# A graph and mixing layer with routed experts: group sizes, early row addresses and unused TensorE products between its two halves

## The chip, the cores and the metric

The kernel runs on one core of one Trainium2 chip. The metric is the device time of one execution in microseconds (us). The engines named below are TensorE (PE), VectorE (DVE), ScalarE (ACT), GpSimd (POOL) and SyncE (SP), which only issues transfers here. Engines wait for one another on semaphores: `x.wait_ge(s, v)` stops engine x until semaphore s has reached v.

## The reference

```python
xn = layernorm(x)                                    # x: 6250 x 256
x = x + gnn(xn, edges) + mix(xn)                     # graph part; linear attention of 8 heads
f = layernorm(x)
logits = softmax(relu(f @ rw1 + rb1) @ rw2 + rb2)    # 6 experts
top_w, top_i = top_k(logits, 2); w = softmax(top_w)
e_out = three layers of 256 x 256 per expert (relu, relu, none), with biases
x = x + sum over the 2 chosen experts of w * e_out
```

## The kernel before

The 6250 rows lie as 50 tiles of 125 rows. The **mixing part** goes through them in 25 pairs. For pair i TensorE forms the mixing product (`mix`), DVE adds the graph rows and x (`mixed_rows`, L1027), and the layernorm and the router follow on ACT, PE and DVE over the next four steps of the loop. Pairs are collected in seven **groups**, `SIZES = (4, 5, 4, 4, 3, 3, 2)`. When the last pair of a group is through the router, DVE chooses the two experts of each of its rows and ranks them (`route`, in four parts: part 0 two steps after that pair, parts 1 and 2 three steps after it, part 3 four steps after it; between parts 2 and 3 TensorE sums the ranks, `ranks`). Part 3 ends with the positions of the rows (L1094, L1095). POOL then writes each tile of the group, 125 rows, to its place in a table `tab0` sorted by expert: one indirect transfer (**scatter**, L588) for each tile, so two for each pair. So groups 4, 5 and 6 (counted from 0) end with pairs 19, 22 and 24 and are 6, 6 and 4 scatters.

After the last group TensorE forms the counts of rows per expert (L1341), DVE turns them into ends of regions (`fill`, L1124) and into two lists, first for the table of first choices, then for that of second choices: the first row of each block of 128 rows (`tab_row`, L1140, signalled as `tab_done`) and its expert (`tab_e`, L1142, signalled as `e_done`). SP writes seven blocks of empty rows behind the regions, six of them after `fill` is ready (`fill_up`, L474).

The **expert part** takes blocks of 128 rows, two to a step, 27 steps for first choices and 27 for second choices. For each block SP reads its address from `tab_row` into a register (`value_load`, L488) and issues the transfer of its rows (L497) into one of 14 buffers; semaphore `r_in` tells that both blocks have landed. ACT normalises them (L775), PE turns them (transposes, L1351), ACT and DVE split them into a high and a low half (L790, L1170), and PE computes the three layers of a step, each two blocks of six products (L1359 to L1361), layers of neighbouring steps interleaved. DVE adds biases (L1150) and weights the result (L1158). POOL writes the rows of a first-choice step into the second table (`second_rows`, L599, two transfers) and adds the results to the output (`add_rows`, L610, two transfers). POOL's order is written out: `second_rows` of steps 0 to 7, then `add_rows(n)` and `second_rows(n + 8)` in turn. Before SP issues the rows of step 27, the first of the second choices, it waits for the last `second_rows`.

Before its first rows SP waits in this order: for the first list (`tab_done`), for the empty blocks of the first table (`fill_out[0]`), and for the scatters and the output writes of the last four groups. It issues nothing else in between.

Of the kernel before, what the change touches and what calls it, by code (L numbers as in the profile page):

```python
# [16 lines left out]
E, F, RH = 6, 256, 128  # L17
# [14 lines left out]


Q = 10
SIZES = (4, 5, 4, 4, 3, 3, 2)
ENDS = tuple(sum(SIZES[:g + 1]) for g in range(len(SIZES)))
GROUPS = len(SIZES)
RB = 4
# [4 lines left out]
HB = 2  # L43
REG = N + S
# [28 lines left out]
def tiles_of(g):  # L73
    return range(2 * (ENDS[g] - SIZES[g]), 2 * ENDS[g])


def gps_layer(nc, x, src, dst, w_kv, w_q, w_oT, b_out, w_g, a_l, a_r, rw1, rb1, rw2, rb2,
              ew1, eb1, ew2, eb2, ew3, eb3, out):
    ctx = ExitStack()
    with ctx:  # L80
        def sb(name, shape, dt=FP32):
            return ctx.enter_context(nc.sbuf_tensor(name, shape, dt))

        def sem(name):
            return ctx.enter_context(nc.semaphore(name))
# [44 lines left out]
        mix_h, mix_l = wg_h[:, :, 0:D], wg_l[:, :, 0:D]  # L130
# [79 lines left out]
        tab_row = sb("tab_row", [1, 2, NTT], I32)  # L210
# [30 lines left out]
        d_ps = ctx.enter_context(nc.psum_tensor("d_ps", [128, 512], FP32))  # L241
# [49 lines left out]
        sc_out, x2_out = [sem(f"sc_out{b}") for b in range(RB)], [sem(f"x2_out{b}") for b in range(RB)]  # L291
        we_in, be_in, b3_in = sem("we_in"), sem("be_in"), sem("b3_in")

        cnt_done, tstep, tab_done, e_done, fill_out = sem("cnt_done"), sem("tstep"), sem("tab_done"), sem("e_done"), [sem(f"fill_out{k}") for k in range(2)]
        fill_ready, second_out = sem("fill_ready"), [sem(f"second_out{c}") for c in range(CB)]
        r_in = [sem(f"r_in{u}") for u in range(U)]
# [23 lines left out]
        def scattered(g):  # L320

            return 16 * sum(2 * SIZES[a] for a in range(g % RB, g + 1, RB))

        def stored(g):

            return 32 * sum(SIZES[a] for a in range(g % RB, g + 1, RB))

# [9 lines left out]
        def expert_regs(engine, name):  # L337
            return [[engine.alloc_register(f"{name}{h}_{i}") for i in range(EL * HB)] for h in range(SETS)]
# [14 lines left out]
        def has(n):  # L353
            return 0 <= n < ALL

        def added(n):

            return z_out[n % YB], 16 * HB * (n // YB + 1)

        def copied(n):  # L360

            return second_out[n % CB], 16 * HB * (n // CB + 1)
# [5 lines left out]
        def _(sp):  # L368
# [100 lines left out]
            def fill_up(k):  # L469
                tab = (tab0, tab1)[k]  # L470
                sp.load(end_regs, fill[0:1, k, 0:E])
                for reg in end_regs:
                    end = sp.snap(reg, min_val=0, max_val=(E - 1) * REG + N)
                    sp.dma_start(tab[bass.ds(end, S), :], skip_rows[:, :]).then_inc(fill_out[k], 16)  # L474

            fill_up(0)
            sp.wait_ge(tab_done, 1)
            sp.wait_ge(fill_out[0], 16 * (E + 1))
            for g in range(GROUPS - RB, GROUPS):
                sp.wait_ge(sc_out[g % RB], scattered(g))  # L480
                sp.wait_ge(x2_out[g % RB], stored(g))

            for n in range(ALL):
                k, j = n // PAIRS, n % PAIRS
                if n == PAIRS:
                    sp.wait_ge(tab_done, 2)
                for h in range(HB):
                    first = sp.value_load(tab_row[0:1, k, j * HB + h:j * HB + h + 1], min_val=0, max_val=E * REG)  # L488
                    if h == 0 and n >= U:
                        sp.wait_ge(*added(n - U))  # L490
                        if n - U < PAIRS:
                            sp.wait_ge(*copied(n - U))
                    if n == PAIRS and h == 0:
                        sp.wait_ge(fill_out[1], 16 * (E + 1))
                        for m in range(PAIRS - CB, PAIRS):
                            sp.wait_ge(*copied(m))
                    sp.dma_start(rb[n % U][:, h, :], (tab0, tab1)[k][bass.ds(first, S), :]).then_inc(r_in[n % U], 16)  # L497
                if n == U - 1:
                    fill_up(1)
# [4 lines left out]
        def _(pool):  # L504
# [80 lines left out]
            for g in range(GROUPS):  # L585
                pool.wait_ge(row_ready, g + 1)
                for j in range(2 * SIZES[g]):
                    pool.indirect_dma_start(out=tab0, out_offset=bass.IndirectOffsetOnAxis(ap=pos0[:, g % RB, j:j + 1], axis=0),  # L588
# [595 lines left out]
        def _(pe):  # L1184
# [159 lines left out]
            pe.wait_ge(we_in, 32 * E)  # L1344
            pe_e = expert_regs(pe, "pe_e")

            def turned(outp, rows):

                for h in range(HB):
                    for c in range(KC):  # L1350
                        last = pe.transpose(outp[:, h, c, :], rows[:, h, c * 128:(c + 1) * 128], ident[:, :])  # L1351
                return last

            def expert_layer(outp, layer, hi, lo, e):

                at = e * EW + layer * LW
                for c in range(KC):
                    w = bass.ds(at + c * F, F)
                    pe.matmul(outp, hi[:, c, :], we_h[:, w], start=c == 0, stop=False)  # L1359
                    pe.matmul(outp, hi[:, c, :], we_l[:, w], start=False, stop=False)  # L1360
                    last = pe.matmul(outp, lo[:, c, :], we_h[:, w], start=False, stop=c == KC - 1)  # L1361
                return last

            def step(n, es):
                if has(n):
                    pe.wait_ge(in_l_done, n + 1)
                    for h in range(HB):
                        last = expert_layer(l1_ps[:, h, :], 0, in_h[:, h, :, :], in_l[:, h, :, :], es[n, h])
                    last.then_inc(l1_done, 1)
                if has(n - 1):  # L1370
                    pe.wait_ge(h1_l_done, n)
                    for h in range(HB):
                        last = expert_layer(l2_ps[:, h, :], 1, h1_h[:, h, :, :], h1_l[:, h, :, :], es[n - 1, h])
                    last.then_inc(l2_done, 1)
                if has(n + 1):
                    pe.wait_ge(xe_done, (n + 2) * HB)
                    turned(tin_ps, xe[:, (n + 1) % 2, :, :]).then_inc(tin_done, 1)
                if has(n):
                    pe.wait_ge(hs1_done, (n + 1) * HB)
                    turned(th1_ps, hs1).then_inc(th1_done, 1)  # L1380
                if has(n - 2):
                    m = n - 2
                    pe.wait_ge(h2_l_done, m + 1)
                    if m >= 2:
                        pe.wait_ge(y_done, (m - 1) * HB)
                    for h in range(HB):
                        last = expert_layer(l3_ps[m % 2][:, h, :], 2, h2_h[:, h, :, :], h2_l[:, h, :, :], es[m, h])
                    last.then_inc(l3_done, 1)
                if has(n - 1):
                    pe.wait_ge(hs2_done, n * HB)  # L1390
                    turned(th2_ps, hs2).then_inc(th2_done, 1)

            tiles(pe, pe_e, step)


# [28 lines left out]
```

## Time and profile before

| | us |
|---|---|
| median of 3 runs | 745.61 (744.7 to 746.4) |
| the profiled execution's own time | 744.4 |
| its span, first to last instruction | 742.6 |

```profile
PE 666.2 (90%) x4705; PEld 615.6 (83%) x4705; DVE 555.0 (75%) x1427; ACT 446.1 (60%) x879; POOL 449.4 (61%) x392
PE   3999999999999988988874299999999999999993
PEclk9999999999999999899985599999999999999998
```

The first line gives busy time, share of the span and instructions of each engine. The other two cut the span in 40 slices of 18.6 us: tenths of busy time of PE (9 is 90% or more), and the TensorE clock that was granted, in tenths of full speed. Before the two low slices lies the mixing part, behind them the expert part.

### The profile page before, as it was taken

Reading aid. Unit: us, or ns where it says so; the run is one execution under the profiler, and the core shown is the slowest. Engines: PE = TensorE matmul, PEld = TensorE weight load, DVE = VectorE, ACT = ScalarE, POOL = GpSimd, SP = SyncE. Lnnn points to the kernel's source line nnn. Section 1 sums busy time; section 2 is a strip of 40 time slices with the busy share of each in tenths; the row PEclk is TensorE's granted clock in tenths of the full one; section 3 lists DMA queues with packets and bytes.
Section 4 is the critical chain, followed back from the end, with each engine's and each line's share of the span. In section 5 each row is a group of like instructions: output and inputs, shape, how many; then the busy total and the mean of one; then the engine's idle time right before and its main releaser. Section 6 shows DMA issues by size and latency. Waiting matters only on the chain.

```text
span 742.6 us, 15734 instructions
## 1 busy us (share of the span) xinstructions
PE 666.2 (90%) x4705; PEld 615.6 (83%) x4705; DVE 555.0 (75%) x1427; ACT 446.1 (60%) x879; POOL 449.4 (61%) x392
## 2 busy tenths in 40 slices
PE   3999999999999988988874299999999999999993
PEld 2888888888888777867663289999999999999993
DVE  5785788888888787678777167777777777777773
ACT  2666577777777547567771166566566566656651
POOL 3465788766666200535466478888888865555555
PEclk9999999999999999899985599999999999999998
DMA  8954544444443367768554578666646965554443
GB/s 229 270 159 145 164 130 125 129 123 122 123 125 110 111 226 241 238 212 267 186 137 115 142 201 187 133 122 119 111 83 108 173 112 95 88 94 60 46 46 36
DMA packets 80759, 104.79 MB, mean 141 GB/s; under 512 B 21156, under 2 KB 62456, under 8 KB 80679
## 3 DMA queue, kind: packets, MB, share of 16 engines
q1 hardware_dynamic: 48135, 70.98, 32.2%
q0 software_dynamic: 32544, 32.80, 25.3%
q8 instruction: 43, 0.70, 0.4%
q14 instruction: 37, 0.30, 0.2%
HBM read 53.35 MB, written 52.26 MB: 142 GB/s over the span
## 4 chain that ended last, share of the span: by engine, by line
PE 79%; DVE 10%; ACT 3%; POOL 2%; issue 2%; DMA 2%; SPq 1%; POOLq 0%; DVEq 0%; ACTq 0%
PE kv_ps L1359 10%; PE kv_ps L1360 10%; PE kv_ps L1361 10%; PE pt L1351 6%; PE d_ps L1223 6%; PE kv_ps L1200 5%; PE kv_ps L1203 5%; PE kv_ps L1201 5%; PE xt_ps L1351 3%; PE kv_ps L1300 2%; PE pt L1200 2%; PE pt L1203 2%; PE pt L1201 2%; POOL tab L588 1%; PE pt L1291 1%
## 5 line engine op out<-in xcount | busy, mean ns | idle before, releaser
L1359 PE MATMUL kv_ps<-we_h,now_h 128*128 x648 | 192.7, 297 | 3.6 <-DVE now_l L1170 2.0
L1360 PE MATMUL kv_ps<-we_l,now_h 128*128 x648 | 183.5, 283 | 0.0
L1361 PE MATMUL kv_ps<-we_h,now_l 128*128 x648 | 183.5, 283 | 0.0
L1359 PEld LDWEIGHTS kv_ps<-we_h,now_h 128*128 128x128 f32 x648 | 124.2, 192 | 5.0 <-issue 5.0
L1360 PEld LDWEIGHTS kv_ps<-we_l,now_h 128*128 128x128 f32 x648 | 124.5, 192 | 0.0
L1361 PEld LDWEIGHTS kv_ps<-we_h,now_l 128*128 128x128 f32 x648 | 124.0, 191 | 0.0
L1150 DVE TENSOR_TENSOR work<-kv_ps,be 128x256 f32<-128x256 f32 x216 | 81.5, 419 | 50.5 <-PE kv_ps L1361 50.1
L610 POOL DMA_INDIRECT out_x<-work,arena x56 | 87.6, 1565 | 39.7 <-DVE work L1158 26.9
L790 ACT ACTIVATE now_h<-pt 128x512 fp32r<-128x512 f32 x54 | 32.5, 602 | 103.3 <-PE pt L1351 103.3
L556 POOL DMA_INDIRECT alg<-xt_tab,src_all x50 | 63.1, 1261 | 38.9 <-DVE arena L939 17.4
L962 DVE TENSOR_REDUCE ss<-xring 125x16 f32<-125x1040 f32 x50 | 61.8, 1236 | 19.9 <-ACT xring L675 18.3
L559 POOL DMA_INDIRECT arena<-xt_tab,dst_all x50 | 61.5, 1230 | 15.2 <-issue 15.2
L1223 PEld LDWEIGHTS d_ps<-work 125*128 125x128 f32 x400 | 52.0, 191 | 4.8 <-DVE work L976 0.9
L1170 DVE TENSOR_TENSOR now_l<-pt,now_h 128x512 fp32r<-128x512 f32 x54 | 37.3, 691 | 23.5 <-ACT now_h L790 23.4
L775 ACT ACTIVATE staged<-arena 128x256 f32<-128x256 f32 x80 | 43.5, 597 | 18.5 <-DMA arena<-tab 18.5
L588 POOL DMA_INDIRECT tab<-work,pos x14 | 16.9, 1206 | 62.1 <-DVE work L1095 58.4
L1223 PE MATMUL d_ps<-work 125*128 125x128 f32 x400 | 52.5, 275 | 0.7 <-DVE work L976 0.7
L599 POOL DMA_INDIRECT tab<-arena x40 | 40.3, 1008 | 21.0 <-issue 10.7
L1200 PE MATMUL kv_ps<-wkv_h,x_h 128*128 128x512 f32 x120 | 49.7, 414 | 0.6 <-ACT arena L648 0.6
L588 POOL DMA_INDIRECT tab<-arena,pos x24 | 28.8, 1200 | 32.9 <-DVE arena L1095 26.5
L1351 PE MATMUL pt<-ident,staged 128*128 128x128 f32 x216 | 33.3, 278 | 16.9 <-ACT staged L775 16.9
L1201 PE MATMUL kv_ps<-wkv_l,x_h 128*128 128x512 f32 x120 | 47.0, 392 | 0.0
(253 smaller groups left out, 1826.4 us busy)
## 6 DMA issues: line engine op xcount, KB each, us to landing
arena<-tab SPq DMA_DIRECT2D x80, 131.0 KB, 3.1
xring<-in_x SPq DMA_DIRECT2D x29, 224.0 KB
we_h<-wt_h SPq DMA_DIRECT2D x6, 768.0 KB, 6.0
we_l<-wt_l SPq DMA_DIRECT2D x6, 768.0 KB, 8.6
xt_tab<-arena SPq DMA_DIRECT2D x7, 577.5 KB
weight_in<-tab SPq DMA_DIRECT2D x28, 131.0 KB, 2.6
out_x<-arena SPq DMA_DIRECT2D x12, 224.0 KB
staged<-in_ew SPq DMA_DIRECT2D x9, 256.0 KB, 4.6
```

The lines of the kernel that those rows point to most:

```text
L556: pool.indirect_dma_start(out=alg[:, b, t % CH, :], out_offset=None, in_=xt_tab, in_offset=bass.IndirectOffsetOnAxis(ap=src_all[:, t:t + 1 ...
L559: pool.indirect_dma_start(out=xtg[:, b, t % CH, :], out_offset=None, in_=xt_tab, in_offset=bass.IndirectOffsetOnAxis(ap=dst_all[:, t:t + 1 ...
L610: pool.indirect_dma_start(out=out, out_offset=bass.IndirectOffsetOnAxis(ap=rb[u][:, h, C_TOK:C_TOK + 1].bitcast(I32), axis=0), in_=yw[n % ...
L962: dve.reduce_sum(ss[:, t % 2, :], sq[t % 2], axis=AX.X).then_inc(red_done, 1)
L1150: dve.tensor_tensor(rows[:, h, :], outp[:, h, :], be[layer][:, bass.ds(es[n, h] * F, F)], ALU.add).then_inc(finished, 1)
L1200: pe.matmul(outp, x_h[:, t, c, :], w_h(c), start=c == 0, stop=False)
L1201: pe.matmul(outp, x_h[:, t, c, :], w_l(c), start=False, stop=False)
L1223: last = pe.matmul(d_ps[:, at], vs[t % VB][:, at], ks[t % VB][:, at], start=False, stop=t == T - 1, skip_group_check=True)
L1351: last = pe.transpose(outp[:, h, c, :], rows[:, h, c * 128:(c + 1) * 128], ident[:, :])
L1359: pe.matmul(outp, hi[:, c, :], we_h[:, w], start=c == 0, stop=False)
L1360: pe.matmul(outp, hi[:, c, :], we_l[:, w], start=False, stop=False)
L1361: last = pe.matmul(outp, lo[:, c, :], we_h[:, w], start=False, stop=c == KC - 1)
```

## The change

The groups become `(4, 5, 5, 4, 3, 2, 2)`: group 2 has five pairs in place of four, and group 5 two in place of three, so groups 2, 3 and 4 end one pair later than before and groups 5 and 6 as before. SP reads the addresses of the first two blocks before its waits for the last scatters. TensorE issues products whose result nobody reads: 40 when the first list of experts is ready, 24 when the scatters of the last group have landed, 8 when the rows of step 0 have landed, and 10 behind the transposes of step 0. They have 128 x 128 weights and 256 columns, the shape of the mixing part's and the layers' products, and write the upper half of the bank `d_ps`.

```diff
-SIZES = (4, 5, 4, 4, 3, 3, 2)
+SIZES = (4, 5, 5, 4, 3, 2, 2)
...
             sp.wait_ge(fill_out[0], 16 * (E + 1))
+            early = [sp.value_load(tab_row[0:1, 0, h:h + 1], min_val=0, max_val=E * REG) for h in range(HB)]
             for g in range(GROUPS - RB, GROUPS):
                 sp.wait_ge(sc_out[g % RB], scattered(g))
                 sp.wait_ge(x2_out[g % RB], stored(g))
...
-                    first = sp.value_load(tab_row[0:1, k, j * HB + h:j * HB + h + 1], min_val=0, max_val=E * REG)
+                    first = early[h] if n == 0 else sp.value_load(tab_row[0:1, k, j * HB + h:j * HB + h + 1], min_val=0, max_val=E * REG)
...
             pe.wait_ge(we_in, 32 * E)
             pe_e = expert_regs(pe, "pe_e")
 
+            def idle_products(count):
+
+                for i in range(count):
+                    pe.matmul(d_ps[:, F:2 * F], wg_h[:, 0, 0:128], mix_h[:, 1, :], start=True, stop=True)
+
+            pe.wait_ge(e_done, 1)
+            idle_products(40)
+            pe.wait_ge(sc_out[(GROUPS - 1) % RB], scattered(GROUPS - 1))
+            idle_products(24)
+            pe.wait_ge(r_in[0], 16 * HB)
+            idle_products(8)
+
...
                     turned(tin_ps, xe[:, (n + 1) % 2, :, :]).then_inc(tin_done, 1)
+                if n < 0:
+                    idle_products(10)
                 if has(n):
```

## Rows read from the trace of the kernel before

**Rows 1.** Busy time by stretch: us, busy (instructions) per engine, granted clock, DMA share.
```profile
386.00:398.00 12.00, 9.61 (x33) 7.30 (x33) 6.75 (x36) 6.38 (x14) 6.68 (x6) 0.56 0.61 168
408.00:420.80 12.80, 0.00 (x0) 0.02 (x1) 2.62 (x9) 1.09 (x2) 3.70 (x4) 0.50 0.47 121
420.80:428.00 7.20, 5.51 (x23) 4.72 (x24) 1.54 (x4) 2.17 (x4) 5.44 (x6) 0.50 0.64 180
429.00:440.00 11.00, 10.59 (x88) 10.12 (x88) 7.74 (x16) 7.54 (x17) 7.89 (x9) 1.00 0.73 205
```

**Rows 2.** Chain of work that ended last: start us, us, what.
```profile
395.46 0.27 DVE rk L1091
...
396.94 1.18 POOL tab L588
...
410.63 4.71 DMA tab<-weight_in,pos
415.49 0.28 SPq L488
...
416.28 0.37 SPq L497
...
417.43 2.06 DMA arena<-tab
419.57 1.10 ACT staged L775 x2
...
420.81 1.10 PE pt L1351 x4
...
424.04 0.21 PE kv_ps L1360
...
430.43 0.12 PE kv_ps L1359
...
431.87 0.45 PE pt L1351 x4
```

**Rows 3.** TensorE in order of time: start us, us, line, tile, idle before.
```profile
423.46 0.58 PE L1359 MATMUL kv_ps<-we_h,now_h 128*128 x1 [1.57 <-DVE now_l L1170]
...
428.74 0.38 PE L1359 MATMUL kv_ps<-we_h,now_h 128*128 x1 [0.29 <-DVE now_l L1170]
```

**Rows 4.** DVE in order of time, end of the mixing part and the lists.
```profile
326.78 0.69 DVE L1027 TENSOR_TENSOR arena<-kv_ps,y 125x512 f32<-125x512 f32 x1
...
384.00 0.69 DVE L1027 TENSOR_TENSOR weight_in<-kv_ps,y 125x512 f32<-125x512 f32 x1
...
388.52 0.21 DVE L1069 TENSOR_REDUCE tw<-kv_ps 125x6 f32<-125x48 f32 x1 [2.58 <-PE kv_ps L1315]
...
404.23 0.16 DVE L1124 CAST fill<-d_ps 1x16 int32<-1x16 f32 x1
...
408.09 0.63 DVE L1142 TENSOR_SCALAR tab_e<-gsum_sb 1x54 int32<-1x54 f32 x1
```

**Rows 5.** POOL in order of time: group 4's first scatter, steps 0 and 26.
```profile
384.18 1.19 POOL L588 DMA_INDIRECT tab<-work,pos  x1 [4.71 <-DVE work L1095]
...
420.31 1.01 POOL L599 DMA_INDIRECT tab<-arena  x1 [8.49 <-DMA arena<-tab]
...
562.42 1.01 POOL L599 DMA_INDIRECT tab<-weight_in  x1 [0.30 <-issue]
```

**Rows 6.** SP's empty blocks in order of time, and the last one's landing.
```profile
406.04 3.68 SPq L474 DMA_DIRECT2D tab<-skip_rows  x6
...
L474 SPq DMA_DIRECT2D tab<-skip_rows x1: 772/772/772, 409.0 to 409.0; - x1
DMA to landing us min/median/max: 4.1/4.1/4.1
```

**Rows 7.** Step 27's rows on ACT, and what TensorE's weight loads waited for.
```profile
568.87 1.09 ACT L775 ACTIVATE staged<-weight_in 128x256 f32<-128x256 f32 x2 [1.25 <-DMA weight_in<-tab]
...
572.07 0.42 PEld L1351 LDWEIGHTS pt<-ident,work 128*128 128x128 f32 x4 [0.20 <-DVE work L1150]
```

## The prediction

> **What bounds the kernel now.** I read first the busy time by stretch [rows 1]: from 408.00 to 420.80 us TensorE does nothing, from 420.80 to 428.00 it works at a granted clock of 0.50, and from 429 on it is busy without a break at 1.00. So the change aims at a hole of some 17 us in which TensorE waits, and at 7 us at half speed behind it. The chain of waits [rows 2] says what fills the hole: the first scatter of group 5 starts at 396.94, the last of group 6 at 410.63, ten without a break, and the last one lands 4.71 us after its start, at 415.34. Then SP reads an address (415.49), issues (416.28), and the second block's transfer starts at 417.43, 1.94 us after the first read. It lands at 419.49, ACT takes 1.10 us, and TensorE's transposes start at 420.81.
>
> Last I looked for what else could set the end, and found POOL. From its first `second_rows` at 420.31 to the last one at 562.42 [rows 5] it works through 27 `second_rows` and 19 `add_rows` with hardly more than its 0.30 us between two transfers. SP can load step 27 only behind that last one, and ACT waits 1.25 us for these rows; DVE falls behind with it, and TensorE's weight loads wait 0.20 us for DVE [rows 7]. **TensorE has no reserve there.** What TensorE gains beyond what POOL gains is paid back at step 27.
>
> **Part 1, the groups.** Group 5 loses two scatters of 1.5 us ((410.63 - 396.94) / 9 = 1.52). That isn't a gain of 3.0, since group 4 now ends a pair later: its part 3 moves from ahead of the 25th pair's L1027 (384.00) to behind it. Of the steps moved for groups 2 and 3, I add up the intervals between the twelve L1027 from 326.78 to 384.00 [rows 4] in the new order of plain and routing pairs: 57.5 in place of 57.2 us, so the last pair starts 0.24 later, at 384.24. On TensorE its ranks now stand directly ahead of the router products that DVE waited for until 388.52, so I take the ranking for 388.3, and the first scatter follows 1.48 us behind the ranking (395.46 to 396.94, rows 2), at 389.8. Before it was at 384.18 [rows 5]. From there the queue is full: 14 scatters, 13 x 1.50 = 19.5, and 0.25 for those that SP's issues slow down. The last starts at 409.55 and lands 4.7 later, at 414.25: **1.1 us earlier**. Bounds: nothing (group 4 or 6 late by 1.1) and 3.0 (both scatters saved whole).
>
> What that move costs: DVE's hole of 2.58 us ahead of 388.52 [rows 4] hid nothing before; now the ranks go ahead of these router products on TensorE, and part 3 ahead of part 0 of group 5 on DVE. Part 0 comes up to 1.2 later; parts 1 to 3 of group 5 with four rows in place of six give back about 0.5. I take 0.7 us for everything behind: the ends (404.23), the list of experts (408.09 + 0.63, so 409.4 in place of 408.7) and the empty blocks; bounds 0.2 and 1.5. Group 6's scatters are ready at 404.2 and POOL comes to them at 404.8, so this doesn't show there.
>
> **Part 2, the addresses.** Both reads leave the way behind the last landing. From the first read to the second transfer's issue it was 1.94 us; left are two issues of 0.37 each, some 0.5. But the reads stand behind the wait for the empty blocks. Their last issue is at 409.0 and lands at 413.1 [rows 6]; 0.7 later is 413.8. Two reads (0.79 from the first one's start to its issue, of which I take 0.6 for the read itself) end at 415.0, and that is behind the scatters' landing at 414.25. So this wait takes the place of the one removed: issues at 415.2 and 415.65, against 417.43: 1.8 earlier. If the scatters gained nothing, the issues would be at 415.5 and 416.0, 1.4 earlier: the sum hardly hangs on part 1. Two blocks of 128 rows in flight together may land later than one behind the other; I take 0.2 (0 to 1.0; a block to its landing takes 2.06 in rows 2, and an empty one amid scatters 4.1 in rows 6). Step 0's rows land at 417.9: **POOL starts 1.6 us earlier** (0.8 to 2.6). Later blocks are issued in the old rhythm behind these, earlier with them.
>
> **Part 3, the products.** At half clock one takes 0.21, at full clock 0.12 [rows 2]. In the trace it is at 0.50 until 428.00 [rows 1], and step 1 at 428.74 is the first at full clock, so it rose some 4.7 us behind the first layer product (423.46, rows 3). The 40 start at 409.4: 4.7 / 0.21 = 22 at half clock, 18 x 0.12 = 2.2 at full, end at 416.3 (bounds 4.8 and 8.5 us for all 40: 414.2 and 417.9). The scatters have landed by then. 24 x 0.12 = 2.9: 419.2. The rows have landed too. 8 x 0.12 = 1.0: 420.2. ACT would have been ready at 419.1, so **the products themselves hold the first transposes back by 1.1 us**, to 420.2, 0.6 ahead of before. The ten behind them (1.2 us at full clock, 2.1 at half) lie in the gap until DVE's `now_l`, 1.57 idle us [rows 3] and the 0.6 by which the transposes get shorter: nothing (if the clock were half: up to 0.5).
>
> What full clock gives: four transposes 0.45 for 1.10, so 0.5 with what overlaps; from the first layer product of step 0 to that of step 1 5.28 us (423.46 to 428.74). At full clock that is twelve products 1.4, four transposes to their end 0.6, and the 1.57 that TensorE waits for ACT and DVE behind such transposes: 3.6, so 1.7 less. TensorE's gain is 0.6 + 0.5 + 1.7 = 2.8 us (1.2 to 4.5).
>
> **The sum.** TensorE gains 2.8, POOL 1.6. At step 27 the smaller one holds: ACT's wait grows from 1.25 to 2.4, TensorE waits 1.2 more, and **1.6 us** are left at the end. From the profiled 744.4 that is 742.8. The median of the runs is 1.2 us above the profiled one, and they spread over 1.7. A run in which the first steps stay longer at half clock passes that on to its end before, and doesn't after, since TensorE has 1.2 of reserve there; I count 0.3 us for it. 745.6 - 1.9 = **743.7 us**.
>
> A rule of the Trainium skill weighs on part 3. The row from 386 to 398 [rows 1] shows TensorE busy 9.6 of 12 us, with transposes and narrow products, at 0.56 of its clock, so busy time alone doesn't bring it back. "TensorE: Matmul & The Clock Gate", Part 4, says that transposes don't count as activity for the full clock; the trace agrees. By this rule the ten products are needed, and the clock could fall at the first transposes if they were too few.
>
> **Rivals.**
> - *TensorE's whole gain reaches the end.* For it: the wait at step 27 is only 0.20 on TensorE. Against it: that is because the two paths are level. It gives 745.6 - 2.8 - 0.3 = 742.5.
> - *The waits ahead of the first rows eat it.* Group 4's late part 3 moves the lists and the empty blocks by 1.5 and not 0.7, the reads end at 415.8, the two transfers land 0.6 apart from my figure: POOL gains 0.4, the end with it: 745.0.
> - *The clock falls again between the last products and the layers.* Then 2.2 of TensorE's 2.8 are gone, TensorE's path is the later one, and 0.6 is left: 745.0. For it: the mean of 0.56 from 386 to 398 [rows 1] shows that it fell where TensorE was busy with transposes and narrow products. Against it: the gaps are now filled.
> - *Slower: the unread products run at half clock to their end.* 82 of them are in front of the first layer. 72 x 0.21 = 15.3 from 409.4 on end at 424.7, 3.9 behind the 420.81 of before, and nothing comes back from the clock: 745.6 + 3.9 = 749.5. It decides once the first transposes start behind 423.2 (420.81 + 2.4, what the full clock gives and the 0.20), and it needs that products of one shape on one weight don't wake the clock. Against it: twelve layer products of this shape, with two tiles of transposes, did.
> - *The change doesn't do what it says* in part 1, since POOL's queue stays full: counted above, it costs 0.4 and not the result.
>
> **Chances.** Forecast (POOL's gain holds, 1.2 to 2.6) 0.57; TensorE's whole gain 0.10; eaten by waits 0.17; clock falls again 0.06; slower 0.08 by the products, and 0.02 by more disturbance of the mixing part than I count (to 747). About 0.2%, 1.5 us, can be told from no change. Of the forecast a good fifth lies under 1.5 us. Faster: 0.45 + 0.10 = 0.55; same: 0.12 + 0.17 + 0.05 = 0.34; slower 0.11. The range takes the forecast, TensorE's gain with its upper bound, and both cases at 745.0: 741.8 to 745.6.
>
> **What would show it.** Right: last scatter from 409 to 410; first transfer of rows at 415.2 behind a landing at 414.3; the 72 products in one block from 409.4, the clock at 1.00 within it, the first transposes at 420.2, straight behind the products with ACT done 1.1 earlier; 3.6 us between the first layers; at step 27 an ACT wait of 2.4 and TensorE idle over 1 us. Wrong: first transposes straight behind ACT, scatters of group 6 that wait for DVE, or no idle TensorE at step 27, with the end 2.8 earlier.

## The result and the profile after

| | before | after |
|---|---|---|
| median of 22 runs each, us | 745.82 (742.98 to 749.14) | 743.33 (739.04 to 747.30) |
| ratio, 95% interval | | 0.9965 (0.9952 to 0.9978) |
| the profiled execution's own time, its span | 744.4, 742.6 | 742.97, 741.1 |

The kernel is 2.5 us faster (1.6 to 3.6 by the interval of the ratio). Between the two profiled executions the difference is only 1.4 us (1.5 in the span). 0.49 us of what is missing lies ahead of the change: the first `mixed_rows` starts at 267.52 in place of 267.03. So what the change itself did, seen in the traces, is 1.9 to 2.0 us. Each of these is a single execution, and executions differ without the change too: from the first `mixed_rows` to the last pair's it took 116.97, 117.98, 118.00 and 118.32 us in the four traces with the old groups (before, f2, e5, f3 below).

The page of after. In the 40 slices of 18.5 us one low slice of PE and of its clock is left where there were two:

```profile
PE 675.8 (91%) x4787; PEld 625.0 (84%) x4787; DVE 555.3 (75%) x1427; ACT 445.8 (60%) x879; POOL 448.1 (60%) x392
PE   2999999999999989888975899999999999999993
PEclk9999999999999999899785899999999999999998
```

Busy time by stretch of after, with the columns of [rows 1]; the last three lines cut the products' stretch into pieces of 2 us:

```profile
386.00:398.00 12.00, 10.19 (x36) 8.12 (x36) 7.57 (x44) 6.51 (x13) 6.01 (x6) 0.50 0.54 166
408.00:420.00 12.00, 9.91 (x68) 9.94 (x69) 4.16 (x13) 1.09 (x2) 3.29 (x4) 0.74 0.53 149
420.00:428.00 8.00, 6.76 (x53) 6.09 (x52) 2.83 (x5) 4.10 (x9) 5.75 (x7) 1.00 0.63 185
...
412.00:414.00 2.00, 2.00 (x11) 2.00 (x11) 0.44 (x2) 0.00 (x0) 0.00 (x0) 0.50 0.57 168
414.00:416.00 2.00, 2.00 (x18) 2.00 (x17) 0.00 (x0) 0.00 (x0) 0.00 (x0) 0.91 0.02 7
416.00:418.00 2.00, 2.00 (x20) 2.00 (x19) 0.00 (x0) 0.00 (x0) 0.00 (x0) 1.00 0.46 134
```

TensorE was idle from 408.00 to 420.80 before and at 0.50 until 428.00 [rows 1]. Now it is busy from 410.09, its clock rises from 0.50 to 1.00 behind 414 with nothing but unread products running, and it is at 1.00 for all of the first steps. TensorE in order of time, step 0 and step 1 (the last line is the first layer of step 1, the one before it that of step 0):

```profile
410.09 10.58 PE L1351 MATMUL d_ps<-wg_h 128*128 128x256 f32 x72 [4.93 <-DVE tab_e L1143]
420.51 0.60 PE L1364 MATMUL pt<-ident,staged 128*128 128x128 f32 x4
420.86 1.42 PE L1351 MATMUL d_ps<-wg_h 128*128 128x256 f32 x10
422.67 0.38 PE L1372 MATMUL kv_ps<-we_h,now_h 128*128 x1 [0.39 <-DVE now_l L1171]
...
426.35 0.38 PE L1372 MATMUL kv_ps<-we_h,now_h 128*128 x1 [0.31 <-DVE now_l L1171]
```

The 72 products form one block; both waits between them were over when TensorE came to them. The first layers are 3.68 us apart, against 5.28 [rows 3].

POOL of after in order of time: group 4's first scatter, the last scatter, the first and the last `second_rows` (answers to [rows 5]):

```profile
390.46 1.19 POOL L589 DMA_INDIRECT tab<-work,pos  x1 [4.99 <-DVE work L1096]
...
409.86 1.18 POOL L589 DMA_INDIRECT tab<-weight_in,pos  x1 [0.30 <-issue]
...
419.15 1.01 POOL L600 DMA_INDIRECT tab<-arena  x1 [8.10 <-DMA arena<-tab]
...
560.93 1.01 POOL L600 DMA_INDIRECT tab<-weight_in  x1 [0.30 <-issue]
```

Then what SP waited for between the list and the first rows (us in total, times, longest), and the landing time of the last scatter:

```profile
SPq L478 <- DMA tab<-skip_rows: 3.3, 1, 3.3
...
DMA to landing us min/median/max: 5.2/5.2/5.2
```

The wait that ends last is named anew: before it was for the scatters, now it is for the empty blocks. The scatters landed at 409.86 + 5.2 = 415.06, while SP was still reading addresses; it issues at 415.67 and 416.2. Last, ACT of after in order of time, the first rows and steps 26 to 28:

```profile
418.41 1.09 ACT L776 ACTIVATE staged<-arena 128x256 f32<-128x256 f32 x2 [16.11 <-DMA arena<-tab]
...
564.37 0.60 ACT L791 ACTIVATE now_h<-pt 128x512 fp32r<-128x512 f32 x1 [1.92 <-PE pt L1364]
...
567.41 1.09 ACT L776 ACTIVATE staged<-weight_in 128x256 f32<-128x256 f32 x2 [1.95 <-DMA weight_in<-tab]
...
569.99 0.60 ACT L791 ACTIVATE now_h<-pt 128x512 fp32r<-128x512 f32 x1 [0.20 <-PE pt L1364]
...
576.48 0.60 ACT L791 ACTIVATE now_h<-pt 128x512 fp32r<-128x512 f32 x1 [1.91 <-PE pt L1364]
```

ACT's wait for step 27's rows grew from 1.25 [rows 7] to 1.95. The second and the third `now_h` are 6.49 us apart; elsewhere in the expert part it is 5.61 to 5.62 a step. Here 0.87 us is paid back. The chain of work that ended last confirms it; it now runs through the last `second_rows`, SP's reads, the rows and ACT (start us, us, what):

```profile
560.93 2.13 DMA tab<-weight_in
563.29 0.33 SPq L498
...
564.39 3.00 DMA weight_in<-tab
567.41 0.06 ACT staged L776
...
568.41 0.58 ACT now_h L799
569.02 0.54 DVE now_l L1179
...
570.61 0.66 PE pt L1364 x4
```

### The profile page after: what moved, and what is told of

Read it like the earlier page. It is cut to its first block, busy times and chain, and to the rows that moved or that the text cites. A ratio compares the mean times of both kernels' runs of the same rounds, so it can differ in the third digit from the quotient of the medians.

```text
span 741.1 us, 15899 instructions
## 1 busy us (share of the span) xinstructions
PE 675.8 (91%) x4787; PEld 625.0 (84%) x4787; DVE 555.3 (75%) x1427; ACT 445.8 (60%) x879; POOL 448.1 (60%) x392
## 4 chain that ended last, share of the span: by engine, by line
PE 74%; DVE 13%; issue 4%; POOL 4%; ACT 3%; DMA 2%; SPq 0%; POOLq 0%; ACTq 0%; DVEq 0%
PE kv_ps L1372 9%; PE kv_ps L1373 9%; PE kv_ps L1374 9%; PE d_ps L1224 6%; PE kv_ps L1201 5%; PE pt L1364 5%; PE kv_ps L1204 5%; PE kv_ps L1202 5%; PE xt_ps L1364 3%; POOL out_x L611 2%; PE pt L1201 2%; PE pt L1204 2%; PE pt L1202 2%; PE kv_ps L1301 2%; PE d_ps L1351 1%
## 5 line engine op out<-in xcount | busy, mean ns | idle before, releaser
L1179 DVE SCALAR_TENSOR_TENSOR now_l<-xt_ps,now_h 128x512 fp32r<-128x512 f32 x54 | 37.4, 692 | 12.4 <-ACT now_h L799 12.4
L676 ACT ACTIVATE xring<-kv_ps 125x512 f32<-125x512 f32 x60 | 35.1, 590 | 13.3 <-PE kv_ps L1204 12.8
```

## The experiments

The theory (the expectations call it theory A or the POOL theory): TensorE starts early enough, POOL's first `second_rows` starts 1.6 us earlier, and the smaller of the two gains survives step 27. The main rival (theory B, but for e1, where B is that two scatters are saved whole): the whole gain of TensorE reaches the end. Three kernels do one part alone, and others take away what each theory says is the limit. No run has the groups and the addresses without the products; what that leaves open is said behind the experiments.

To compare traces I use a mark in each that lies behind the mixing part: the start of the count product (L1341 before, L1342 after), 403.33 before and 404.56 after. The times count from it, in us, one profiled execution each. "Steps 0 to 1", "steps 1 to 2" and "at step 27" are the distances of `now_h` on ACT (without a wait it is 5.61 at step 27), "end" is the last step's `now_h`. Where the rows of step 27 came very late, the distance ahead of the one in the column is long too: 6.75 in f3, 5.77 in f2, 5.72 in e8, 5.66 in e6.

The mark isn't free of the change. From the last pair's L1027 (L1028) to it takes 19.23 to 19.33 us with the old groups and 19.83 to 19.86 with the new ones. So beside a row with the old groups, every time of a row with the new ones looks 0.5 to 0.6 us earlier than it is. Rows with the same groups compare as they stand.

| kernel | last scatter | first `second_rows` | `now_h` of step 0 | steps 0 to 1 | steps 1 to 2 | at step 27 | end | ratio of times, 95% |
|---|---|---|---|---|---|---|---|---|
| before | 7.30 | 16.98 | 18.60 | 5.35 | 5.06 | 5.79 | 314.94 | 1 |
| groups (f1) | 5.31 | 15.22 | 16.84 | 5.35 | 6.79 | 5.62 | 315.07 | 0.9975 (0.9953 to 0.9996) |
| addresses (f2) | 7.22 | 15.80 | 17.42 | 5.31 | 5.08 | 6.80 | 314.89 | 0.9989 (0.9967 to 1.0011) |
| products (f3) | 7.30 | 17.12 | 18.23 | 3.71 | 5.06 | 8.53 | 317.10 | 1.0004 (0.9984 to 1.0025) |
| **after** | 5.30 | 14.59 | 16.58 | 3.75 | 5.08 | 6.49 | 312.25 | 0.9965 (0.9952 to 0.9978) |
| before, AHEAD 10 (e5) | 7.29 | 16.84 | 18.47 | 5.34 | 6.89 | 5.61 | 316.58 | 1.0004 (0.9984 to 1.0025) |
| after without the ten (e6) | 5.30 | 14.97 | 16.51 | 3.70 | 5.07 | 6.83 | 312.42 | 0.9966 (0.9947 to 0.9984) |
| after, 40 more (e7) | 5.30 | 14.87 | 20.68 | 3.70 | 5.07 | 5.61 | 315.25 | 1.0006 (0.9991 to 1.0021) |
| after, reads first (e8) | 5.29 | 14.46 | 16.13 | 3.72 | 5.09 | 6.80 | 312.12 | 0.9961 (0.9946 to 0.9976) |
| e8, 14 for 24, AHEAD 10 (f4) | 5.32 | 14.16 | 15.74 | 3.70 | 5.07 | 5.61 | 310.31 | 0.9935 (0.9913 to 0.9957) |

Each ratio is against runs of before on the same chip, and is not just the quotient of the medians (for f4 that would be 0.9954). The medians of before there were 745.8, 746.3 (e5 to e8) and 745.2 (f1 to f4).

### The parts one by one, on a chip with stalls of its own (e1, e2, e3, e4)

e1, the groups alone:

```diff
-SIZES = (4, 5, 4, 4, 3, 3, 2)
+SIZES = (4, 5, 5, 4, 3, 2, 2)
```

> Theory A (POOL's unbroken queue from its first rows to the last transfer into the second table carries the gain to the end, and what TensorE gains beyond it is paid back at step 27): groups alone bring POOL's first rows forward only by what the last scatter lands earlier. The changed kernel's trace has 0.3 us of that (415.05 against 415.34), since the last landing took 5.2 us in place of 4.7; so 0.3 to 1.1 us faster. Theory B (two scatters of 1.5 us are saved whole): 3 us faster.

Measured: 767.95 us against 768.91 of before, ratio 0.9983 (0.9962 to 1.0005).

e2, the addresses alone:

```diff
             sp.wait_ge(fill_out[0], 16 * (E + 1))
+            early = [sp.value_load(tab_row[0:1, 0, h:h + 1], min_val=0, max_val=E * REG) for h in range(HB)]
...
-                    first = sp.value_load(tab_row[0:1, k, j * HB + h:j * HB + h + 1], min_val=0, max_val=E * REG)
+                    first = early[h] if n == 0 else sp.value_load(tab_row[0:1, k, j * HB + h:j * HB + h + 1], min_val=0, max_val=E * REG)
```

> Both theories: the two reads leave the way behind the last landing, 1.94 us from the first read to the second issue become some 0.6. The empty blocks land at 413.1 with the old groups, so the reads end at 414.3, ahead of the scatters' landing at 415.3, and are hidden whole. POOL and TensorE both start 1.3 to 1.4 us earlier, TensorE's first steps stay at half clock, and the end is 1.4 us earlier (0.19%).

Measured: 767.39, ratio 0.9983 (0.9968 to 0.9997).

e3, the products alone:

```diff
+            pe.wait_ge(e_done, 1)
+            idle_products(40)
+            pe.wait_ge(sc_out[(GROUPS - 1) % RB], scattered(GROUPS - 1))
+            idle_products(24)
+            pe.wait_ge(r_in[0], 16 * HB)
+            idle_products(8)
...
+                if n < 0:
+                    idle_products(10)
```

> Theory A: the first layers of steps 0 and 1 are 3.7 us apart in place of 5.3 and TensorE is 2 us ahead, but POOL's first rows stay where they were; ACT's wait at step 27 grows from 1.2 to about 3 us, TensorE waits 2 us there, and the end is 0 to 0.3 us earlier. Theory B: TensorE sets the end, so it comes 2 us earlier (0.3%).

Measured: 769.15, ratio 1.0032 (1.0006 to 1.0057).

e4, after with POOL's last `second_rows` two steps further ahead of the additions, which takes away what POOL does to step 27:

```diff
-AHEAD = 8
+AHEAD = 10
```

> The changed kernel with ten in place of eight steps of rows moved into the second table ahead of the first addition to the output (AHEAD). The last of these transfers is then issued two additions of two transfers earlier, some 7.5 us. Theory A: ACT no longer waits for step 27's rows, TensorE keeps its surplus of the first steps, and the end is 0.9 to 1.2 us earlier than that of the changed kernel, 3 to 3.7 us earlier than before by the medians (0.4 to 0.5%). Theory B (step 27 doesn't matter): as the changed kernel, ratio 0.9965.

Measured: 769.21, ratio 1.0002 (0.9983 to 1.0021), where after had 0.9965 on its own chip. After itself wasn't run here.

These four don't decide. Every kernel, before too, took 3% longer on this chip, and the loss sits in the expert part ahead of step 27: in e1 and e4 the steps up to about the 24th are mostly 5.6 to 8 us apart, and from there on 5.61. Three lines of e4, of ACT, DVE and POOL, from the first steps of the expert part:

```profile
434.36 0.60 ACT L791 ACTIVATE now_h<-pt 128x512 fp32r<-128x512 f32 x1 [9.99 <-remote]
...
433.72 0.76 DVE L1151 TENSOR_TENSOR work<-kv_ps,be 128x256 f32<-128x256 f32 x2 [9.54 <-remote]
...
457.73 1.61 POOL L611 DMA_INDIRECT out_x<-work,arena  x1 [6.94 <-DVE work L1159]
```

ACT and DVE stood for nearly 10 us each in the same stretch (DVE's wait at this place is 2.04 us in after), which the profile puts down to no wait of the kernel's own ("remote"). The first two steps of e4 took 11.57 and 12.47 us in place of 3.7 and 5.1, and POOL's additions began late behind them. What comes early into such stalls can be lost in them; that it was lost isn't shown. So the parts were run again on another chip, with before beside them.

### What holds the end: POOL's order, without the change (e5)

```diff
-AHEAD = 8
+AHEAD = 10
```

on before.

> The kernel before with AHEAD = 10 alone. Theory A: in the profiled execution of before the two paths were level (TensorE's loads waited 0.20 us at step 27), so 0.2 us come out, more in executions whose first steps reach full clock earlier: 0 to 0.7 us faster. If step 27 doesn't matter: no change.

Measured: 746.38 us, ratio 1.0004 (0.9984 to 1.0025). The wait at step 27 went (5.61), and no time with it: before had only 0.18 us there. A gain of 0 to 0.7 us and none at all can't be told apart here, so this run doesn't part the theories. The trace showed something else that bears on the sum. Two stretches of 1 us of e5, columns as in [rows 1]:

```profile
432.00:433.00 1.00, 1.00 (x6) 1.00 (x6) 0.76 (x2) 0.00 (x0) 0.82 (x1) 0.50 0.83 225
433.00:434.00 1.00, 1.00 (x9) 1.00 (x9) 0.00 (x0) 0.00 (x0) 0.69 (x2) 0.92 0.69 166
```

In this execution TensorE got its full clock only at 433, in before's at 428 [rows 1]. Steps 1 to 2 took 6.89 us in place of 5.06, and the end is 1.64 later than in before. So without the products a late clock costs 1.8 us, and nothing later absorbs it.

### The ten products behind the transposes (e6)

```diff
-                if n < 0:
-                    idle_products(10)
```

> The changed kernel without the ten products behind the first transposes. If the clock needs them it falls to 0.50 behind the transposes of step 0, the first layers of steps 0 and 1 are 5.3 us apart in place of 3.7, TensorE loses 1.6 us of its lead of 1.3 over POOL, and the end is 0.3 us later than that of the changed kernel. If a hole of 1.6 us between products is short enough, the clock stays at 1.00 and nothing changes: ratio 0.9965.

Measured: 743.71, ratio 0.9966 (0.9947 to 0.9984), the same as after. Two stretches of e6 and the first layer of step 0 in order of time:

```profile
420.00:422.00 2.00, 0.43 (x4) 0.25 (x3) 0.69 (x1) 1.57 (x3) 1.68 (x2) 1.00 0.68 211
422.00:424.00 2.00, 1.89 (x16) 1.65 (x15) 0.39 (x2) 0.07 (x1) 1.39 (x3) 1.00 0.71 192
...
421.76 0.38 PE L1372 MATMUL kv_ps<-we_h,now_h 128*128 x1 [1.57 <-DVE now_l L1171]
```

TensorE did four transposes and then nothing for 1.57 us, and its clock stayed at 1.00. The ten products aren't needed here, and within the interval they cost nothing.

### Forty products more (e7)

```diff
-            idle_products(40)
+            idle_products(80)
```

> The changed kernel with 80 products in place of 40 in the first group. At full clock the forty more take 4.8 us, so the first transposes start at 425.3. Theory A: TensorE's lead of about 0.7 to 0.9 us over POOL at step 27 swallows that much, the rest reaches the end: 3.9 to 4.1 us later than the changed kernel, 1.5 to 2.5 us slower than before. ACT doesn't wait at step 27. Rival (TensorE sets the end throughout): 4.8 us later.

Measured: 746.06, ratio 1.0006 (0.9991 to 1.0021): the whole gain is gone, 3.1 us against after (0.41%), where I had expected 3.9 to 4.1. TensorE and POOL of e7 in order of time:

```profile
409.38 14.70 PE L1351 MATMUL d_ps<-wg_h 128*128 128x256 f32 x112 [4.91 <-DVE tab_e L1143]
...
441.62 1.61 POOL L611 DMA_INDIRECT out_x<-work,arena  x1 [2.23 <-DVE work L1159]
```

The block is 4.1 us longer, not 4.8. Step 0's `now_h` is 4.1 later than in after, and the end 3.0. After's loss at step 27 (0.87) isn't there in e7, and an interval at step 6 that is 0.23 too long in after is 0.08 too long; these had absorbed the rest. So TensorE has a reserve of about 1.1 us in after, and of the delay beyond it all reached the end. A second thing shows: POOL's first addition waited 2.23 us for step 0's result. POOL can't use an early start beyond that point unless TensorE is early enough too.

### The addresses ahead of the wait for the empty blocks (e8)

```diff
-            sp.wait_ge(fill_out[0], 16 * (E + 1))
             early = [sp.value_load(tab_row[0:1, 0, h:h + 1], min_val=0, max_val=E * REG) for h in range(HB)]
+            sp.wait_ge(fill_out[0], 16 * (E + 1))
```

> The changed kernel with the two early reads ahead of the wait for the empty blocks. There the reads ran from 414.1 to 415.2, behind the empty blocks' landing, and the scatters landed at 415.05: the reads ended 0.15 us late, and the first issue came at 415.67. Moved ahead they are hidden whole: first issue at 415.3 to 415.5, POOL and the end 0.2 to 0.4 us earlier. If the way from the landing to the issue is SP's own passing of its eight waits, nothing changes.

Measured: 743.09, ratio 0.9961 (0.9946 to 0.9976). What SP waited for in e8:

```profile
SPq L481 <- DMA tab<-weight_in,pos: 2.4, 1, 2.4
```

Now the scatters are the last wait again. SP issues 0.32 us behind their landing (415.07 and 415.39), in after 0.61 behind it. The first `second_rows` and the end are 0.13 earlier, less than the 0.2 to 0.4 expected. The mechanism is in the trace; its size is beneath what the medians tell.

### The parts again, on the chip of e5 to e8 (f1, f2, f3)

f1 is the kernel of e1.

> Groups alone once more, on another chip than e1_groups (there every kernel was 3% slower and its first steps took 7 us and more). POOL theory: step 0's rows land 0.3 to 0.8 us earlier, and the end comes as much earlier: 0.04 to 0.1%. If two scatters were saved whole: 3 us (0.4%).

Measured: 743.66, ratio 0.9975 (0.9953 to 0.9996), 1.9 us (0.3 to 3.5), against the 0.3 to 0.8 expected. Against the count the last scatter is 2.0 earlier and the first `second_rows` 1.76; with the mark's own shift of 0.5 taken off, that is 1.5 and 1.26. But its profiled execution is one of the late ones of the clock. One stretch and POOL in order of time:

```profile
429.00:430.00 1.00, 1.00 (x6) 1.00 (x6) 0.05 (x1) 0.02 (x1) 0.76 (x1) 0.50 0.77 243
...
440.87 1.61 POOL L610 DMA_INDIRECT out_x<-work,arena  x1 [2.10 <-DVE work L1158]
```

The clock is still at 0.50 at 430, steps 1 to 2 took 6.79 us, and the first addition waited 2.10 us for step 0. So this trace, like e5's, has lost what its start had gained: its end is 0.6 later than before's, counted from the last pair. What the part is worth is said by the 12 runs, and only within that wide interval; the trace says why it varies.

f2 is the kernel of e2.

> Addresses alone once more. POOL and TensorE both start 1.3 to 1.4 us earlier; the end 1.4 us earlier (0.19%). ACT's wait for step 27's rows stays at 1.2 us or less in the trace.

Measured: 745.01, ratio 0.9989 (0.9967 to 1.0011): 0.8 us, 1.4 expected, and unclear against zero. The reads are hidden (first issue 0.27 us behind the last landing, 0.95 before), and the first `second_rows` is 1.18 earlier. ACT at step 27:

```profile
571.57 1.09 ACT L776 ACTIVATE staged<-weight_in 128x256 f32<-128x256 f32 x2 [2.41 <-DMA weight_in<-tab]
```

ACT's wait is 2.41, not the 1.2 or less expected. From the last `second_rows` to these rows it took 7.89 us here, 6.45 in before and 6.48 in after, and that 1.4 us took the gain of this one execution. It lies mostly in the landing of the last `second_rows`, here in f2's chain of work:

```profile
563.68 3.41 DMA tab<-weight_in
```

In after the same transfer took 2.13, and the rows behind it took about the same time in both (3.13 and 3.00). Why it landed late is open. Load on the transfer engines wasn't the reason: from 564 to 567 their busy share was 0.00 to 0.09.

f3 is the kernel of e3. It is the one that parts the two theories: TensorE gains 2 us, POOL nothing.

> Products alone once more. POOL theory: POOL's first rows stay at 420 us, TensorE's lead of 1.6 to 2 us is paid back at step 27 (interval of that step 7.2 to 7.6 us in place of 5.6), so a profiled execution gains 0 to 0.3 us on that of before; by the medians 0 to 0.15%, since executions whose clock rises late gain. If TensorE's clock carries the gain: 2 us (0.27%), interval of step 27 5.6 to 5.8.

Measured: 746.29, ratio 1.0004 (0.9984 to 1.0025): no gain. That TensorE's whole gain reaches the end is refuted: 2 us would be 0.9973, outside the interval. Its trace at step 27 shows more than a gain paid back; ACT and TensorE in order of time, then stretches of 2 us:

```profile
570.91 1.09 ACT L775 ACTIVATE staged<-weight_in 128x256 f32<-128x256 f32 x2 [3.40 <-DMA weight_in<-tab]
...
572.05 0.66 PE L1363 MATMUL pt<-ident,staged 128*128 128x128 f32 x4 [0.49 <-ACT staged L775]
...
574.46 1.11 PE L1363 MATMUL pt<-ident,work 128*128 128x128 f32 x4 [1.75 <-DVE work L1150]
...
572.00:574.00 2.00, 0.66 (x4) 0.42 (x4) 1.05 (x3) 1.76 (x4) 1.70 (x2) 1.00 0.99 181
574.00:576.00 2.00, 1.54 (x7) 1.55 (x8) 1.66 (x5) 0.40 (x1) 1.62 (x2) 0.54 1.04 166
576.00:578.00 2.00, 2.00 (x13) 2.00 (x13) 0.72 (x2) 1.18 (x3) 1.56 (x1) 0.61 0.91 187
578.00:580.00 2.00, 2.00 (x20) 2.00 (x18) 1.59 (x4) 1.39 (x3) 1.59 (x2) 1.00 1.05 186
```

The lead over POOL became a hole on TensorE of 0.49 and 1.75 us with only transposes between, and the granted clock fell to its lower level: 0.54 and 0.61 are the means of two stretches of which part was at 1.00. From step 27's rows on ACT to the end it is 151.14 us here, and 149.40 to 149.44 in before, after, e6, e8 and f2. So the low clock cost 1.7 us more than the lead itself. In e6 and f2 ACT's wait was 2.30 and 2.41, and there was no such loss. The end of f3 is 2.2 later than before's; the other 0.4 is that step 27's rows came 0.42 later, although POOL's last `second_rows` was 0.36 earlier.

The three parts alone make 0.25% + 0.11% - 0.04% = 0.32%, the whole 0.35%: within the intervals they add up. But groups and addresses alone make 0.36% already, so these runs don't show that the products add anything to the change.

### A version that should beat both (f4)

After, with all that the runs pointed to: the addresses read first (e8), fewer products ahead of the first transposes, and no wait for POOL at step 27.

```diff
-AHEAD = 8
+AHEAD = 10
...
-            idle_products(24)
+            idle_products(14)
```

> The changed kernel with the reads ahead of the wait for the empty blocks, 14 in place of 24 products in the second group (first transposes no longer held back by 1 us), and AHEAD = 10 (the last transfer into the second table some 7.5 us earlier). POOL theory: no wait at step 27 (0.9 to 1.3 us kept), rows 0.2 us earlier, transposes 0.9 us earlier: 2.0 to 2.4 us faster than the changed kernel, 0.6% faster than before. If step 27 doesn't matter: 1 us faster than the changed kernel at most.

Measured: 741.77 (9 runs, 738.89 to 742.34), ratio 0.9935 (0.9913 to 0.9957). Its median is 3.5 us below that of before beside it, where after's was 2.5 below; by the ratios it gained 0.30%, 2.2 us, more than after. The two intervals overlap by 0.0005. ACT at step 27 in order of time:

```profile
569.63 0.60 ACT L791 ACTIVATE now_h<-pt 128x512 fp32r<-128x512 f32 x1 [1.92 <-PE pt L1364]
...
570.60 1.09 ACT L776 ACTIVATE staged<-arena 128x256 f32<-128x256 f32 x2
...
575.24 0.60 ACT L791 ACTIVATE now_h<-pt 128x512 fp32r<-128x512 f32 x1 [1.92 <-PE pt L1364]
```

No wait for rows is left, and the steps are 5.61 apart. The end is 1.94 earlier than in after: 0.84 from step 0's earlier start, 0.87 from step 27, 0.23 from the hiccup at step 6. AHEAD alone did nothing in e5, since TensorE hadn't the lead that it sets free. The three edits weren't run one by one, so this split is read from one trace.

## Why the prediction was right

It said 743.7 (741.8 to 745.6), and it is 743.3. The path was as forecast: POOL's gain is what reaches the end, and TensorE's surplus is paid back at step 27. That the median came within 0.4 us is partly luck, since executions of one kernel spread over 6 us and more. Step by step, where 0.49 of every time of after is the later start of that run:

- **The order of the mixing part.** The last pair's L1028 starts at 384.73, 0.73 later than in before. Less 0.49 that is the 0.24 worked out from the intervals; this close a match is luck, since the same stretch varied by 1.35 us among the traces with the old groups. Everything behind DVE was to be 0.7 later: the experts' list is done at 409.94 against 408.72, 1.2, less 0.49 is 0.7. What varies little is the part behind the last pair, 0.5 to 0.6 later in every trace with the new groups, where the prediction has 0.46.
- **The scatters.** The last starts at 409.86 (409.55 predicted), but lands 5.2 later, not 4.7. This term was mis-sized: I took the landing time of before, whose last scatter stood in a queue of another length. It cost little, since SP was reading addresses until 415.2 anyway.
- **The addresses.** Empty blocks landed at 414.0, reads done at 415.2, issues at 415.67 and 416.2; predicted were 413.8, 415.0, 415.2 and 415.65, again with 0.2 to 0.5 of it the later start. That the wait for the empty blocks takes the place of the one removed was right; e8 shows its size, 0.3 us at the first issue.
- **The products.** One block from 410.09 to 420.67, the clock risen within it, transposes at 420.51 (420.2). ACT was ready at 419.50, so the products did hold them back, by 1.0 (1.1). The first layers are 3.68 apart (3.6).
- **The ten.** They weren't needed: after the transposes and the hole of e6 the clock stayed at 1.00. After transposes between longer holes (f3) it fell to 0.54. The rule weighed in the prediction (the Trainium skill, "TensorE: Matmul & The Clock Gate", Part 4) says that transposes don't count as activity. The prediction took from it that the ten are needed; e6 shows that here they aren't. f3 agrees with the rule but doesn't test it, since TensorE also stood idle there for longer than in e6.
- **Step 27.** TensorE gained 2.39 up to step 1, which is 2.88 with the later start added (2.8 predicted), and POOL 1.16, with it 1.65 (1.6). ACT's wait grew to 1.95 (2.4), 0.87 was paid back by TensorE (1.2), and 1.46 was left, with the later start 1.95 (1.6). POOL gained another 0.3 between its first and last `second_rows`, and that came on top. f3 shows the same step with TensorE alone ahead: none of its 2 us of lead reached the end.
- **The late clock.** I counted 0.3 us for executions whose clock rises late. e5 and f1 show the thing itself, 1.7 to 1.8 us when it happens. The median gained 2.5, the traces 1.95, which leaves 0.55; the interval of the median is as wide as 2 us, so 0.3 is neither confirmed nor refuted. How often the clock rises late isn't known, as each kernel has one trace. The mean granted clock of every execution gives a hint: of the 35 runs of before beside e5 to e8, 18 have 0.951 or less and take 747.2 us in the mean, the other 17 take 745.2 (e5's traced execution has 0.949, before's 0.954). But dips of the clock in the mixing part count in that mean as well, and the runs didn't spread less with the products: before's from 743.0 to 749.1, after's from 739.0 to 747.3.
- **Slips in the sums.** 72 x 0.21 is 15.1, not 15.3, so the slower rival gives 749.3. With TensorE's gain at its stated upper bound of 4.5 the range would start at 741.1, not at 741.8. Neither touches the forecast.

**The rivals.** TensorE's whole gain fell with f3. Waits that eat the gain: the lists moved by 0.7, not by the 1.5 that this needed, and the two first transfers were issued 0.5 apart as worked out. The clock falling between the last products and the layers didn't happen, with or without the ten. The slower rival was to decide once the first transposes start behind 423.2, which is 39.2 behind the last pair's L1027. In e7 they start at 423.92, 39.9 behind it, and by the same mark its end is 0.84 later than before's; its runs can't be told from before's. So the break-even was in about the right place, though the clock rose and the products reached it by their number.

**What I hadn't seen** is how the parts hang together. POOL's first addition waits for step 0's result when POOL starts early and TensorE's first steps don't keep up (2.10 in f1, 2.23 in e7; in before, f2 and after it waited for nothing), and TensorE's lead becomes a hole once POOL starts late (f3). I had taken the two gains as independent, with the smaller one winning. In after POOL is early, TensorE is early by more, and neither effect shows, which is why the sum came out.

**Whether the products do anything in after is not shown.** By the prediction's own sum they needn't: earlier rows bring the first transposes forward too, by the same 1.6 us as POOL, and the rest of TensorE's gain is what step 27 takes back. An estimate from the table: without products `now_h` of step 0 comes 1.62 behind the first `second_rows` (before, f1, f2), and the next two come 5.33 and 5.07 later. From after's 14.59 that puts step 2's at 26.61, where after has it at 25.41. It would be 1.2 later, and after has about 1.1 in reserve (e7). So in an execution like the one traced the products are worth an estimated 0.1 us, and more only where the clock would have risen late. In f4, where step 27 takes nothing back, the same estimate gives 26.18 against 24.51, 1.7 us. The run that would settle it, groups and addresses alone, wasn't made.

## What to carry to other kernels

Where two engines run level, find the step at which the lead of one must be paid back, and count the smaller gain; then look whether the idle time that the lead becomes there lets TensorE's clock fall, since that costs more than was gained (f3). Products that nobody reads can raise the clock in a wait ahead of dense work, if they end when the data are there: forty more than that undid the change, and ten fewer were part of the best version. What they raise is the lead of one engine, so they pay only where nothing later takes it back: alone they gave nothing (f3). And take what the loss at the meeting point names as the next edit: a change of POOL's order that was worth nothing alone (e5) was worth 0.87 us behind this one, by the trace of f4.

## What the runs showed of the hardware

- Unread products of one weight tile, the same operands each time, raise the granted clock like layer products: they start at 410.09, and the stretches of 2 us from 412, 414 and 416 have 0.50, 0.91 and 1.00.
- The moment of the rise varies from execution to execution of nearly the same program: behind 428 in before, behind 430 in f1, at 433 in e5, with the first layer products at 423.46, 421.60 and 423.72. Steps 1 to 2 took 1.7 us (f1) and 1.8 us (e5) longer with the late rise.
- At 1.00, four transposes and 1.57 us of nothing left the clock up (e6). With idle 0.49, four transposes and idle 1.75 the next stretch of 2 us has 0.54 (f3).
- The landing of one and the same indirect transfer, POOL's last into the second table, took 2.13 us in after and 3.41 in f2, at a busy share of the transfer engines of 0.00 to 0.09 in f2.
- One chip ran every kernel 3% slower, with stalls of up to 10 us on DVE and ACT that the profile puts down to no wait of the kernel (e4). What a change gains in such a stretch can't be told there; a second chip was needed.
